# A one-core perceiver layer on Trainium2: self attention's norms by row tile, its stacks by DMA, two of four value tiles inside attention, output banks copied out

## The reference, cut to what matters

```python
Q = split_heads(x @ W_Q.T)            # 512 x 512, 16 heads of 32
K = split_heads(x @ W_K.T)
V = split_heads(x @ W_V.T)
Q = layernorm(Q, q_ln_w, q_ln_b)      # over the 32 of each head, eps 1e-5
K = layernorm(K, k_ln_w, k_ln_b)
attn = softmax(Q @ K.T / sqrt(32))
context = attn @ V
z = context @ sparse_W_V.mean(2)      # then the 128 largest of each head are kept
y = z_sparse @ sparse_W_O.mean(1)
```

## Time and profile before

| what | value |
|---|---|
| median of three runs | 1704.1 us |
| the profiled execution's own time | 1702.76 us |
| its span in the trace | 1701.0 us |
| mean granted TensorE clock | 0.947 |
| TensorE busy | 1551.6 us, 91% |
| VectorE busy | 1197.0 us, 70% |
| ScalarE busy | 969.2 us, 57% |
| GpSimd busy | 373.7 us, 22% |

### The profile page before, as it was taken

One profiled execution on the slowest core, in us unless ns is written; L12 is line 12 of the kernel. 1 busy time (PEld: TensorE's weight loads), 2 busy tenths in 40 slices (PEclk: granted clock), 3 DMA queues, 4 the chain that ended last, 5 costly groups with the idle time before them and its releaser, 6 DMA issues. The chain is left out here.

```text
span 1701.0 us, 21706 instructions
## 1 busy us (share of the span) xinstructions
PE 1551.6 (91%) x7992; PEld 819.7 (48%) x7992; DVE 1197.0 (70%) x1834; ACT 969.2 (57%) x1167; POOL 373.7 (22%) x141
## 2 busy tenths in 40 slices
PE   6799999999999799999999999998877706899998
PEld 4466666666665333333333333333443203777775
DVE  5777677677677799999999999996866384320002
ACT  3366666666666688888888888881444411111110
POOL 4453654654652105030012001001000000100001
PEclk9899999999999899999999999998968757799999
DMA  4454454453453654565454444443110090379993
GB/s 173 153 194 153 145 187 150 159 186 139 171 185 105 156 125 118 138 172 144 116 137 125 124 116 115 118 99 50 26 25 1 7 395 1 118 275 325 327 330 103
DMA packets 117336, 250.26 MB, mean 147 GB/s; under 512 B 9704, under 2 KB 26088, under 8 KB 112752
## 3 DMA queue, kind: packets, MB, share of 16 engines
q1 hardware_dynamic: 115520, 244.68, 46.0%
q0 software_dynamic: 1280, 4.20, 0.8%
q10 hardware_dynamic: 432, 0.01, 0.0%
HBM read 182.26 MB, written 61.34 MB: 143 GB/s over the span
## 5 line engine op out<-in xcount | busy, mean ns | idle before, releaser
L748 ACT ACTIVATE att_pr<-att_sc 128x1024 f32<-128x1024 f32 x512 | 496.2, 1022 | 75.3 <-PE att_sc L665 75.3
L798 DVE TENSOR_TENSOR att_tot<-att_tot,att_pr 128x2048 f32<-128x2048 f32 x200 | 467.1, 2336 | 22.0 <-ACT att_pr L748 1.8
L491 DVE CUSTOM_DVE_ANT_0 ctx_size<-ctx_tot,ctx_size 128x512 f32<-128x512 f32 x512 | 333.0, 688 | 134.6 <-PE ctx_tot L411 130.9
L462 ACT ACTIVATE ctx_size<-ctx_dif 128x1024 f32<-128x1024 f32 x256 | 262.3, 1025 | 125.7 <-PE ctx_dif L411 125.7
L665 PE MATMUL att_sc<-g_stacks,att_kst 98*128 98x512 f32 x1024 | 309.0, 424 | 1.5 <-DVE g_stacks L589 1.5
L665 PEld LDWEIGHTS att_sc<-g_stacks,att_kst 98*128 98x128 f32 x1024 | 173.9, 189 | 236.7 <-ACT att_pr L748 211.5
L679 PE MATMUL att_o<-att_pr,att_val 128*32 128x512 f32 x2048 | 273.6, 606 | 2.0 <-issue 1.9
L1742 ACT ACTIVATE ex_hidT<-ex_hp,m_b 128x128 f32<-128x128 f32 x120 | 34.3, 368 | 185.2 <-PE ex_hp L1697 185.1
L411 PE MATMUL ctx_dif<-ctx_k_dif,f_q_hi 32*128 32x512 f32 x512 | 129.2, 501 | 10.1 <-DVE ctx_best L491 6.1
L411 PE MATMUL ctx_tot<-ctx_k_sum,f_q_hi 32*128 32x512 f32 x512 | 128.4, 498 | 0.0
L86 PE MATMUL f_proj<-f_wv_hi,g_stacks 128*128 128x512 f32 x320 | 120.8, 420 | 0.0
(11 more groups left out here) (269 smaller groups left out, 1974.5 us busy)
## 6 DMA issues: line engine op xcount, KB each, us to landing
m_w<-in_W SPq DMA_DIRECT2D x30, 2048.0 KB, 13.6
att_kst<-keys_scratch SPq DMA_DIRECT2D x192, 256.0 KB, 3.9
f_raw<-in_ctx SPq DMA_DIRECT2D x32, 1024.0 KB, 6.0
keys_scratch<-f_k_hi SPq DMA_DIRECT2D x32, 512.0 KB, 2.8
keys_scratch<-f_k_lo SPq DMA_DIRECT2D x32, 512.0 KB, 3.2
values_scratch<-ctx_v SPq DMA_DIRECT2D x32, 512.0 KB, 3.1
att_val<-values_scratch SPq DMA_DIRECT2D x64, 256.0 KB, 2.6
rows_scratch<-mix_blank SPq DMA_DIRECT2D x1, 3840.0 KB, 26.0
```

Source lines behind the costliest of these rows:

```text
L462: act.activation(size[:, i % ABS, :], dif[:, :], ACT.Abs).then_inc(s_size, 1)
L491: dve.tensor_tensor_reduce(out=size[:, i % ABS, r * CH:(r + 1) * CH], in0=tot[i % 2][:, r * CH:(r + 1) * CH], in1=size[:, i % ABS, r * CH: ...
L748: act.activation(pr[:, T % SLOTS, 2 * s:2 * s + 2, :], sc[(2 * T + s) % PAIRS][:, :].rearrange("p (j q) -> p j q", j=2), ACT.Exp, scale=SC ...
L798: dve.tensor_tensor(tot[b % 2][:, :, :], so_far, pr[:, T % SLOTS, :, :], ALU.add).then_inc(s_add, 1)
```

## The change

In `self_projections` queries and keys become eight row tiles of 128x512, each in its own PSUM bank `raw`. TensorE projects tile n and turns tile n-2 right behind it (float32 transposes back into the tile's own bank); VectorE and ScalarE handle the norm tile by tile. ScalarE writes the high part straight from PSUM as float32r and the full part beside it, VectorE only the low part. The 24 copies into places of the stacks that VectorE and ScalarE did are gone: all 24 (12 for the queries, 12 for the keys) are DMAs issued by SyncE, and those of the keys are cut in two, first head group 0 alone and then groups 1 to 3, 12 and 12 issues. Nothing in the block waits for their landing; TensorE waits at the start of `self_attend` for the first 24, and before its 17th `whole` for the last 12. Only value tiles 0 and 1 are projected in the block; tiles 2 and 3 are projected by 8 float32 matmuls between the first wholes of `self_attend`, into the score banks. The sums of the mixing weights move from VectorE to GpSimd in `self_attend`, by halving additions (`add_up`).

In `self_attend` the shift is one row instead of two (one VectorE instruction after a head instead of three, one row of ScalarE's copy, 97 contracted rows instead of 98). `take` copies den and o to SBUF, so that TensorE's next `weighted` waits for two copies instead of for `normalise`; the division is done later from the copies, in four pieces of 128 columns a head group, one piece after each head's maxima. The last group's division reads PSUM and is in four pieces too. The tile `pr` of the exponentials shares its memory with the low parts.

```diff
+def add_up(pool, out, src, room, s_add, done):
+    half = src.shape[-1] // 2
+    pool.tensor_tensor(room[:, :, 0:half], src[:, :, 0:half], src[:, :, half:], ALU.add).then_inc(s_add, 1)
+    while half > 1:
+        half, done = half // 2, done + 1
+        pool.wait_ge(s_add, done)
+        dst = room[:, :, 0:half] if half > 1 else out.unsqueeze(2)
+        pool.tensor_tensor(dst, room[:, :, 0:half], room[:, :, half:2 * half], ALU.add).then_inc(s_add, 1)
+    return done + 1
...
 def self_projections(nc, c):
...
+        raw = [pb(f"raw{n}", [P, D]) for n in range(TILES)]
...
         def _(sp):
...
+            def key_rows(part, place, groups, done):
+                for j in range(HG):
+                    src, dst = part[HD * j:HD * j + HD, groups, :], c.skst[HD * place:HD * place + HD, j::HG, :][:, groups, :]
+                    sp.dma_start(f32(dst), src).then_inc(done, 16)
+            sp.wait_ge(s_hi, NT)
+            for place in (0, 1):
+                stack_copies(sp, c.stacks, f32(hi[0][:, :, :]), place, c.s_copy[0])
+            sp.wait_ge(s_lo, NT)
+            stack_copies(sp, c.stacks, f32(lo[0]), 2, c.s_copy[0])
+            for groups, done in ((slice(0, 1), c.s_copy[0]), (slice(1, G), c.s_copy[1])):
+                sp.wait_ge(s_hi, TILES)
+                key_rows(f32(hi[1][:, :, :]), 0, groups, done)
+                key_rows(f32(hi[1][:, :, :]), 2, groups, done)
+                sp.wait_ge(s_lo, TILES)
+                key_rows(f32(lo[1]), 1, groups, done)
...
         def _(pe):
...
+            for n in range(TILES):
+                if n == NT:
+                    pe.wait_ge(c.sk_in, 16)
+                project(raw[n], c.swkT if n >= NT else c.swqT, n % NT).then_inc(s_raw, 1)
+                if n >= 2:
+                    turn(n - 2)
             pe.wait_ge(c.sv_in, 16)
...
+            pe.wait_ge(s_hi, 1)
+            pe.wait_ge(s_full, 1)
+            project(raw[0], c.swvT, 0).then_inc(s_v, 1)
+            turn(TILES - 2)
+            pe.wait_ge(s_hi, 2)
+            pe.wait_ge(s_full, 2)
+            project(raw[1], c.swvT, 1).then_inc(s_v, 1)
+            turn(TILES - 1)
...
         def _(dve):
...
+            def spreads(n):
+                dve.wait_ge(s_sq, n + 1)
+                dve.tensor_reduce(spread[:, n % 2, :], heads(sq[:, :]), AX.X, ALU.add).then_inc(s_spread, 1)
+                dve.wait_ge(s_spread, n + 1)
+                if n >= 2:
+                    dve.wait_ge(s_rstd, n - 1)
+                dve.tensor_scalar(std[:, n % 2, :], spread[:, n % 2, :], 1.0 / HD, EPS, ALU.mult, ALU.add).then_inc(s_var, 1)
+            def centre(n):
                 dve.wait_ge(s_raw, n + 1)
-                step(dve.tensor_reduce(total[:, :], heads(raw[:, :, :]), AX.X, ALU.add))
-                step(dve.tensor_scalar(mean[:, :], total[:, :], 1.0 / HD, None, ALU.mult))
-                if n:
-                    dve.wait_ge(s_nrm, n)
-                dve.tensor_tensor(heads(cen[:, :, :]), heads(raw[:, :, :]), wide(mean), ALU.subtract).then_inc(s_cen, 1)
-            def normalise(n):
-                dve.wait_ge(s_sq, n + 1)
-                step(dve.tensor_reduce(spread[:, :], heads(nrm[:, :, :]), AX.X, ALU.add))
-                dve.tensor_scalar(std[:, :], spread[:, :], 1.0 / HD, EPS, ALU.mult, ALU.add).then_inc(s_var, 1)
+                dve.tensor_reduce(total[:, n, :], heads(raw[n][:, :]), AX.X, ALU.add).then_inc(s_total, 1)
+                dve.wait_ge(s_total, n + 1)
+                dve.tensor_scalar(mean[:, n % 2, :], total[:, n, :], 1.0 / HD, None, ALU.mult).then_inc(s_mean, 1)
+                if n >= 3:
+                    dve.wait_ge(s_tp, n - 2)
+                dve.wait_ge(s_mean, n + 1)
+                dve.tensor_tensor(heads(cen[:, n % 3, :]), heads(raw[n][:, :]), wide(mean[:, n % 2, :]),
+                                  ALU.subtract).then_inc(s_cen, 1)
...
+                dve.reciprocal(rstd[:, n % 2, :], std[:, n % 2, :]).then_inc(s_rstd, 1)
+                dve.wait_ge(s_rstd, n + 1)
+                dve.tensor_tensor(heads(cen[:, n % 3, :]), heads(cen[:, n % 3, :]), wide(rstd[:, n % 2, :]),
+                                  ALU.mult).then_inc(s_nrm, 1)
+            def low(n):
+                kind, t = divmod(n, NT)
+                at = slice(t * P, t * P + P)
+                dve.wait_ge(s_hi, n + 1)
+                dve.wait_ge(s_full, n + 1)
+                dve.tensor_tensor(lo[kind][:, :, at], full[:, n % 2, :, :], f32(hi[kind][:, :, at]), ALU.subtract).then_inc(s_lo, 1)
+            centre(0)
+            for n in range(1, TILES):
+                spreads(n - 1)
+                centre(n)
+                scale(n - 1)
+                if n >= 3:
+                    low(n - 3)
+            spreads(TILES - 1)
+            scale(TILES - 1)
+            for n in range(TILES - 3, TILES):
+                low(n)
+            dve.wait_ge(s_lo, TILES)
...
         def _(act):
...
             def affine(n):
-                col = KINDS[n][3]
+                kind, t = divmod(n, NT)
+                col = 2 * kind
+                act.wait_ge(s_tp, n + 1)
+                src = raw[n][:, :].rearrange("p (g q) -> p g q", g=G)
+                act.activation(hi[kind][:, :, t * P:t * P + P], src, ACT.Identity,
+                               scale=c.aff[:, col:col + 1], bias=c.aff[:, col + 1:col + 2]).then_inc(s_hi, 1)
+                if n >= 2:
+                    act.wait_ge(s_lo, n - 1)
+                act.activation(full[:, n % 2, :, :], src, ACT.Identity,
+                               scale=c.aff[:, col:col + 1], bias=c.aff[:, col + 1:col + 2]).then_inc(s_full, 1)
...
+            for n in range(TILES):
                 if n:
...
+                    root(n - 1)
+                square(n)
+                if n >= 2:
+                    affine(n - 2)
+            root(TILES - 1)
+            affine(TILES - 2)
+            act.wait_ge(s_v, 1)
+            act.activation(c.sval[:, 0, :], raw[0][:, :], ACT.Copy).then_inc(s_val, 1)
+            affine(TILES - 1)
+            act.wait_ge(s_v, 2)
+            act.activation(c.sval[:, 1, :], raw[1][:, :], ACT.Copy).then_inc(s_val, 1)
+            act.wait_ge(s_hi, TILES)
+            act.wait_ge(s_val, 2)
...
 def self_attend(nc, c):
...
+        pr = c.own_pr
...
+        held = sb("held", [P, 2, N])
+        s_take = sem("take")
...
         def _(pe):
+            def value_product(n):
+                t, k = 2 + n // DC, n % DC
+                mm = pe.matmul(sc[t - 2][:, :], c.hT[:, k, t * P:(t + 1) * P], c.swvT[:, k, :],
+                               start=(k == 0), stop=(k == DC - 1))
+                if k == DC - 1:
+                    mm.then_inc(s_v, 1)
...
+                pe.wait_ge(s_parts, h + 1)
...
+                    mm = pe.transpose(rows[0:MROW + 1, t * P:(t + 1) * P], shift[:, i:i + MROW + 1], c.ident[:, :])
...
+                pe.matmul(sc[i % 3][:, :], c.skst[0:STK + 1, HG * g + j, u * P:(u + 1) * P],
+                          c.stacks[0:STK + 1, HG * g + j, :], start=True, stop=True).then_inc(s_sc, 1)
...
+                    pe.wait_ge(s_take, 2 * g)
...
             pe.wait_ge(s_set, 1)
+            pe.wait_ge(c.s_copy[0], 16 * HG * 6)
             for i in range(LEAD):
+                if i == STEPS:
+                    pe.wait_ge(c.s_copy[1], 16 * HG * 3)
                 whole(i)
                 if i % NT == NT - 1 and i > NT:
                     turn(i // NT - 1)
+                if 1 <= i <= DC * NT // 2:
+                    value_product(i - 1)
+            pe.wait_ge(s_val, NT // 2)
...
+            def values(t):
+                act.wait_ge(s_v, t - 1)
+                act.activation(c.sval[:, t, :], sc[t - 2][:, :], ACT.Copy).then_inc(s_val, 1)
             for h in range(HG):
+                if h in (1, 2):
+                    values(h + 1)
                 to_rows(h)
...
+        def _(pool):
+            wv, wo = mixing_parts(c)
+            pool.memset(c.mix_bv[:, :], 0.0).then_inc(s_bv, 1)
+            pool.wait_ge(c.mix_in, 16 * 5 * HG)
+            done = add_up(pool, om[:, 0:HD // 2], wo[0], room, s_om, 0)
+            pool.wait_ge(s_om, done)
+            done = add_up(pool, om[:, HD // 2:], wo[1], room, s_om, done)
+            pool.wait_ge(s_om, done)
+            done = add_up(pool, vm[:, :], wv, room, s_om, done)
...
-            def normalise(g):
+            def normalise(g, piece):
+                at = slice(COLS * piece, COLS * piece + COLS)
+                if g < G - 1:
+                    total, values = held[:, 0, at], held[:, 1, at]
+                    dve.wait_ge(s_take, 2 * g + 2)
+                else:
+                    total, values = den[:, at], o[:, at]
+                    dve.wait_ge(s_pv, NT * G)
+                if g == 0 and piece == 0:
+                    dve.wait_ge(s_om, 7)
+                if g >= 1:
+                    dve.wait_ge(s_out, PIECES * (g - 1) + piece + 1)
```

(39 more changed lines are left out.)

204 lines of the change are left out of this document (57 added, 147 removed).

## The result

The changed kernel takes 1682.5 us (median of 4 runs, 1678.7 to 1687.5) where the kernel before, on the same chip, takes 1700.8 (4 runs, 1696.4 to 1704.3). The ratio is 0.9895, 95% interval 0.9852 to 0.9939: faster by 1.1%. Forecast were 1687.0 us, range 1676 to 1698. The base of the forecast, 1704.1, was the median of the first three of those four runs; the fourth, 1696.4, brought the median down to 1700.8.

The account below looks back on a forecast made before the run. TensorE was taken to be held by norm-stage handovers, division waits and its 1.2 GHz clock. Norm -5.1, lead +4.5, loop -16.5 sum to -17.1 us: 1702.8 to 1685.7, median 1.3 higher, 1687; range 1676 to 1698.

Parts of the forecast that it names:

- Norm stage: Up to the first whole: tiles relayed at 3.91 us, then 24 SyncE issues ending the block; -5.1 us.
- the size hardly counts: Norm stage: a copy's issue costs SyncE about 0.67 us at half or full size; 24 issues take 16.9 us.
- The rule that I weighed there: Norm stage: if issue time is small beside the DMA, the block ends soon after 1220, gain 15 us larger.
- Lead: First whole to first score: eight value products come in, 22.6 us against 18.1; +4.5 us.
- the bounds of +2 and +11: Lead: +2 us if TensorE runs at 2.4 GHz from the start, +11 if at 1.2 GHz throughout.
- the one up to the ninth whole and the last value product: Lead: first six us at 1.2 GHz, then pairs of 1.17 us; about 13 us to the ninth whole.
- lead cold: Rival: TensorE stays at 1.2 GHz through the whole lead; +6.5, 1693.5 us; chance 0.16.
- Main loop: Head group ends stop waiting for division; two copies cost 1.4 us twice, last division +0.6; net -16.5 us.
- no drop of the clock there: Sign of being right: TensorE's clock does not fall at a head group's end, no wait above 1.5 us.
- It costs nothing there: Main loop: each divided piece, 1.2 us, fits in VectorE's 1.8 us idle time in a quartet.
- GpSimd's sums: Mixing sums on GpSimd take 20 us, 37 by the slower row, under the main loop; nobody waits before head 10.
- Starved relay: Rival, norm stage: small waits hold TensorE at 1.2 GHz, a tile takes 7.8 us; 1722 us, slower; chance 0.05.

Follow-up runs that it names:

- Unsplit: Changed kernel with 12 key copies of all four head groups instead of 24 split ones, all before the barrier; 1686.3 us, ratio 0.9921.
- late_issues: Changed kernel with the last 12 key copies (head groups 1 to 3) issued behind the barrier instead of before it; 1679.0 us, ratio 0.9881.
- unsplit_act: Unsplit with the four copies of the low part issued on ScalarE's queue instead of SyncE's; 1683.7 us, ratio 0.9911.
- values4: Changed kernel with all four value tiles projected in the norm block and no value product in the lead; 1681.4 us, ratio 0.9898.
- best: Changed kernel with late key copies, ScalarE issuing low-part copies, four value tiles in the norm block, bank copies behind two maxima; 1671.8 us, ratio 0.9843.
- after_again: The changed kernel, unaltered, run again on another chip; 1685.0 us, ratio to the kernel before 0.9913.
- Bank_div: Changed kernel with the bank copies taken back: division in one piece from PSUM, the next products waiting for it; 1696.3 us, ratio 0.9982.
- whole_div: Changed kernel with bank copies kept, but each head group divided in one piece instead of four; 1684.2 us, ratio 0.9913.
- best_again: The same kernel as best, run again beside after_again on one chip; 1669.2 us, ratio to the kernel before 0.9818.
- mix_first: Changed kernel with the mixing sums back on VectorE at the start of the norm block instead of on GpSimd; 1694.7 us, ratio 0.9961.

## Why the prediction was right, point by point

**The whole.** -20.8 us in the stage against -17.1 forecast, 1682.5 against 1687.0, inside the range. No rival came true as a whole. The stage gained 3.7 us more than the sum had. That the medians moved by 18.3 us (1700.8 to 1682.5), nearer to 17.1 than the stage is, is luck: they carry the unchanged parts too, which in the two profiles differ by 6.6 us one way and 3.4 the other.

**Norm stage: right in mechanism, 1.2 us too dear.** The relay ran at 3.88 us a tile (3.91 forecast), the last turn was over 40.6 us behind the start (41.2), and the first issue stood at 41.5 (42.0). The 24 issues took 16.3 us (16.9). One premise of the term was too simple all the same: that "the size hardly counts". It holds for a single issue (0.585 us for the shortest at full size, 0.564 for the shortest at 32x512), not for a row of them: I had taken the median of the four full size issues, 0.66 us; their sum in the timeline, 3.44 us for four, is 0.86 each against 0.67 at half the size, and was there to be read. Here an issue takes 0.62, 0.72 and 0.98 us in the mean for 1, 3 and 4 head groups. The forecast came out because the mean of the first two happens to lie at 0.67. Unsplit shows what that premise would have led to: a gain of 4 to 6 us that is a loss of 1.4. The rule that I weighed there, from the Trainium skill ("DMA: Bandwidth & Descriptors", section "Issuing engines are not separate DMA queues"), says that the issue is usually small beside the DMA. The trace agrees for one copy: median 0.60 us of issue, 3.9 us from issue to landing. The consequence that I gave it, a block that ends soon after 1220, does not follow, since the 24 issues stand in a row in front of the barrier: 12 of them alone held the first whole back by 8.3 us (late_issues). That DMAs of different issuing engines run on the same 16 engines, which the same section says, agrees with unsplit_act, where a second queue brought 0.6 us.

**Lead: the sign right, the size off.** +2.6 instead of +4.5, within the bounds of +2 and +11. The mis-sized term is the one up to the ninth whole and the last value product: 13 us forecast, 11.3 measured (1229.42 to 1240.70). I let 1.2 GHz last six us, by the stretch at 1177. Here the pairs of a whole and a value product go from 2.13 us each to 1.09 at 1234.3, 4.9 us behind the first whole; that is 1.1 us of it, and the quick pairs, 1.09 against 1.17, the rest. The clock also fell again 17.8 us behind the first whole, which the sum did not have. By values4 the lead is 1.4 us shorter without the products; how much they cost and how much clock they give back is not separated there, as GpSimd's additions delay that lead too. The rival "lead cold" is what values4 and best show, but for 19.3 and 18.7 us and not 29, since without value products VectorE, delayed by GpSimd, sets the pace.

**Main loop: right.** -17.1 against -16.5. The copies cost 1.20 us twice (1.4 forecast), nothing at the third place, the last division +0.8 (0.6), and the clock stood at 1.00 from 1254.6 to the end. In after_again it did not: behind the second wait of 1.07 us it fell, and the sign "no drop of the clock there" failed at that place. Bank_div returns 16.4 us alone. "It costs nothing there" of the pieces is borne out by whole_div, 4.5 us when the cover is too short.

**GpSimd's sums:** 22 us, 1229.24 to 1251.5, under the lead and the first scores (20 forecast). That no one waits for their results is right. What the prediction left out is that they delay VectorE: with them one shift took up to 0.35 us in the changed kernel, 0.72 in after_again and 1.2 in values4 and best_again, without them never more than 0.172.

**Starved relay:** it did not come, but the reason that I gave, that TensorE never waits at 1.2 GHz, was only part. VectorE, at 3.89 us, is as full as TensorE; mix_first shows that 7 us of delay in front end as 10.6. I gave 5% to a danger that this one ordering keeps away.

**The profiled execution.** I put the median 1.3 us above the sum, from three runs. That offset hides the spread of the unchanged parts: over the 14 profiles the changed stage starts between 1170.7 and 1179.1, and the rest behind it differs by up to 4.9 us. Neither is in a term.

## What to carry to other kernels

Take an accumulator out of PSUM by two plain copies before a long division, and do the division in pieces that fit the idle time of its engine: here the copies brought 12 us and the pieces 4.5 more. A part of that was TensorE's clock: behind a wait of 4.4 us sixteen products took 3.6 us instead of 1.9. Before a barrier, count the DMA issues that stand in front of it: only those belong there that the first instruction behind it needs. And do not fill an engine in a relay without slack, not even for work that looks free on it; behind the relay, on VectorE, the same work cost nothing. An idle GpSimd is not free either: its additions held up VectorE's short instructions, four of which ended together with the addition beside them.

## What the runs showed of the hardware that I had not expected

- A row of issues of SBUF to SBUF copies lasts longer with their size and with what else is moving: on SyncE in the mean 0.62 us for 32x512, 0.72 for 32x3x512, 0.98 for 32x4x512, 1.05 with ScalarE issuing beside it, whose own took 1.34. The shortest of full size took 0.585.
- A VectorE instruction of 128x4 elements in SBUF took 0.17 us alone and up to 1.66 beside GpSimd's additions. In values4, late_issues, best and unsplit its end follows the end of the addition by 0.03 us (1245.61 after 1245.58 in values4). The maxima of values4, which read PSUM, did not lengthen: 0.674 to 0.693 us.
- These copies hold the sixteen DMA engines at a share of 1.06 while they move 206 GB/s (unsplit, above); the loads from DRAM later in the profiles reach 374 to 391 GB/s at shares of 0.93 to 1.03. A byte of these copies took the engines about twice the time of a byte of those loads.
- After some 10 to 20 us of idle TensorE the lead began at clock 0.50 every time. In best it began after 2.03 us of idle TensorE, at 2.4 GHz, with two wholes in 0.92 us; the next pairs took 1.39, and the windows from 1234 to 1250, wholes at VectorE's pace, read 0.50. With the eight value products between the wholes (changed kernel) the clock was at 1.00 from 4.9 us behind the first whole.
